# Last attention of a four-layer model: row maxima over pairs of banks, one exponential per bank, one output projection for two head groups

## The reference, cut to what matters

```
def _L3_xattn_ref(query, key, value, mask, Wq, bq, Wk, bk, Wv, bv, Wo, bo):
    Q = query @ Wq.T + bq; K = key @ Wk.T + bk; V = value @ Wv.T + bv
    ...
    scores = jnp.einsum('bhqd,bhkd->bhqk', Q, K) / jnp.sqrt(jnp.float32(DK))
    scores = jnp.where(mask == 0, -jnp.inf, scores)
    weights = jax.nn.softmax(scores, axis=-1)
    attn = jnp.einsum('bhqk,bhkd->bhqd', weights, V)
    return attn.transpose(0, 2, 1, 3).reshape(b, -1, D) @ Wo.T + bo
```

## Time and profile before

| | us |
|---|---|
| median of 3 runs (lowest, highest) | 2823.01 (2810.94, 2833.49) |
| the profiled execution | 2821.8 |
| its span, first to last instruction | 2820.0 |

### The profile page before, as it was taken

How to read it: one execution, slowest core, us unless ns; L and a number is a source line. 1 busy time by engine, 2 the same in 40 slices (tenths; PEclk the granted TensorE clock), 3 DMA queues, 4 the chain that set the end, 5 groups by cost and what they waited for, 6 DMA issues and landing times.

```text
span 2820.0 us, 32986 instructions
## 1 busy us (share of the span) xinstructions
PE 2473.9 (88%) x12476; PEld 1269.9 (45%) x12476; DVE 1821.0 (65%) x3631; ACT 1196.4 (42%) x1580; POOL 509.5 (18%) x281
## 2 busy tenths in 40 slices
PE   8999999998767884999897999885999999999878
PEld 3322222223322233778664677663444444443377
DVE  5676777887568766233453244483786888887386
ACT  2343433434345431122441223450365666666753
POOL 0333333333222226200002540000000000000011
PEclk8999999999869997999997999885697999999989
DMA  3000000000020004100102220003130202000042
GB/s 117 1 1 1 1 1 1 1 1 1 12 120 1 0 1 160 59 1 1 37 32 87 82 70 1 4 1 75 42 56 1 36 6 37 6 31 1 1 147 93
DMA packets 47866, 93.49 MB, mean 33 GB/s; under 512 B 7211, under 2 KB 32441, under 8 KB 46681
## 3 DMA queue, kind: packets, MB, share of 16 engines
q1 hardware_dynamic: 47078, 90.22, 10.4%
q10 hardware_dynamic: 628, 1.14, 0.2%
HBM read 79.48 MB, written 11.38 MB: 32 GB/s over the span
## 4 chain that ended last, share of the span: by engine, by line
PE 55%; DVE 13%; ACT 3%; issue 2%; DMA 2%; ACTq 0%; SPq 0%; POOL 0%; DVEq 0%; POOLq 0%
PE PS L2374 7%; PE PS L1297 6%; PE PS L2355 5%; DVE pm L2479 4%; PE PS L2317 4%; PE PS L914 4%; PE PS L1255 2%; PE PS L1278 2%; PE PS L1280 2%; PE PS L1279 2%; PE PS L896 1%; PE PS L2398 1%; PE PS L373 1%; DVE xg L324 1%; PE PS L1072 1%
## 5 line engine op out<-in xcount | busy, mean ns | idle before, releaser
L2479 DVE TENSOR_REDUCE pm<-PS 128x1 f32<-128x512 f32 x768 | 479.3, 684 | 100.5 <-PE PS L2317 100.4
L2445 ACT ACTIVATE P<-PS 128x1024 f32<-128x1024 f32 (+1 forms) x416 | 407.7, 1021 | 213.8 <-PE PS L2355 212.2
L2317 PE MATMUL PS<-Ks,Qs 49*128 49x512 f32 x768 | 314.8, 491 | 41.3 <-DMA Qs<-row 26.5
L682 ACT ACTIVATE P<-PS 128x1024 f32<-128x1024 f32 (+1 forms) x208 | 212.7, 1024 | 319.3 <-PE PS L597 296.5
L714 DVE TENSOR_REDUCE pm<-PS 128x1 f32<-128x400 f32 (+1 forms) x512 | 265.2, 563 | 74.6 <-PE PS L563 72.2
L2355 PE MATMUL PS<-Qs,Ks 51*128 51x512 f32 (+1 forms) x832 | 281.0, 451 | 8.6 <-ACT P L2445 8.6
L2374 PE MATMUL PS<-P,V 128*17 128x512 f32 (+1 forms) x1664 | 231.7, 630 | 0.3 <-ACT P L2445 0.3
L610 PE MATMUL PS<-P,V 128*64 128x512 f32 (+1 forms) x832 | 227.2, 625 | 4.9 <-ACT P L682 4.9
L2355 PEld LDWEIGHTS PS<-Qs,Ks 51*128 51x128 f32 (+1 forms) x832 | 140.5, 191 | 191.3 <-ACT P L2445 148.6
L520 POOL TENSOR_TENSOR odd<-odd,P 128x1024 f32<-128x1024 f32 x64 | 164.6, 2572 | 257.3 <-ACT P L682 257.3
L2317 PEld LDWEIGHTS PS<-Ks,Qs 49*128 49x128 f32 x768 | 136.3, 198 | 138.3 <-DVE pm L2479 91.1
(11 more groups left out here) (343 smaller groups left out, 4673.7 us busy)
## 6 DMA issues: line engine op xcount, KB each, us to landing
mi<-in_mask SPq DMA_DIRECT2D x32, 800.5 KB, 4.4
We<-in_L_ffn_w SPq DMA_DIRECT2D x16, 1024.0 KB, 7.1
Wg<-gate_rows SPq DMA_DIRECT2D x8, 1024.0 KB, 11.8
Qs<-q_parts SPq DMA_DIRECT2D x90, 64.0 KB, 2.4
Ks<-k_parts SPq DMA_DIRECT2D x24, 200.1 KB, 6.5
q_parts<-T SPq DMA_DIRECT2D x7, 512.0 KB, 2.8
k_parts<-Tk SPq DMA_DIRECT2D x6, 400.0 KB, 2.5
X<-in_x SPq DMA_DIRECT2D x4, 512.0 KB, 8.4
```

The source lines that it names most:

```text
L682: e.activation(self.P[0:r, n % 4, :, :], PS[0:r, b:b + 2, :], ACT.Exp, scale=0.125).then_inc(*k.ac_exp.up(("A", n)))
L2317: m = e.matmul(PS[:, b, :], self.Qs[rows, s, pr, q0:q0 + 128], self.Ks[rows, s, pr, cs], start=True, stop=not masked)
L2445: e.activation(self.P[0:r, n % 4, :, :], PS[0:r, b:b + 2, :], ACT.Exp, scale=0.25).then_inc(*k.ac_exp.up((3, n)))
L2479: e.tensor_reduce(self.pm[:, u % 2, i, c:c + 1], PS[:, ring.of(("max", key)), :], AX.X, ALU.max).then_inc(*k.dv_max.up((3, *key)))
```

## The change

- **Maxima over two banks.** The ring becomes `[4, 6]`: a step takes one of two pairs of banks (4 and 5, 6 and 7). Two maxima matmuls of the same `hh` fill a pair, and one VectorE reduction reads 1024 columns: key blocks 0 and 1 of one query block, or key block 2 of two query blocks; `"rest"` pairs likewise (528 columns). The matmuls stay the same in number; VectorE's reductions per unit go from 48 + 4 to 24 + 2. A small step takes a whole pair of banks too.
- **One exponential per bank.** Scores use banks 0, 1 and 2 by turns; each of the four scores of a round has its own exponential of 512 columns, and waits for the exponential three scores earlier. The attend sum moves to bank 3. The order of the scores in a round is now both of `hh = 0`, then both of `hh = 1`.
- **Attend in the middle.** Attend of a round moves from the end of the next round to its middle, between the scores of `hh = 0` and those of `hh = 1`.
- **Projection for two head groups.** The attend results of groups 0 and 1 (2 and 3) are stacked on partitions 0 to 63 and 64 to 127 of `On3`, and `"wo"` runs once for both with 128 rows: 32 steps instead of 64, none in the rounds of units 1 to 4 and 9 to 12. `"back"` uses ordinary float32 matmuls with the identity in place of transposes.
- The prologue ahead of the first round and the slots of the small steps are laid out in blocks of four maxima steps.

```diff
-        self.ring = k.ring([4, 5, 7])
+        self.ring = k.ring([4, 6])
...
+        tiles = [[(pr, qt, c) for c in range(2)] for pr in range(2) for qt in range(4)]
+        tiles += [[(pr, qt, 2) for qt in (q, q + 1)] for pr in range(2) for q in (0, 2)]
+        out = [(self, "max", (u, *x, hh)) for two in tiles for hh in (1, 0) for x in two]
+        return out + [(self, "rest", (u, pr, hh)) for hh in (1, 0) for pr in range(2)]
...
-        out = [(self, "wo", (u, qt)) for qt in range(4)]
+        out = [(self, "wo", (u, qt)) for qt in range(4)] if u // 4 % 2 else []
...
+            slots = spread(weave(*parts), 13)
             for kt in range(KT):
+                for hh in range(2):
+                    for pr in range(2):
+                        out.append((self, "score", (u, kt, pr, hh)))
+                        if done < len(maxima):
+                            out.append(maxima[done])
...
+                    if hh == 0 and before:
+                        out.append((self, "attend", before))
...
+            n = 4 * (13 * u + kt) + 2 * hh + pr
+            rows, ps = slice(64 * hh, 64 * hh + 51), PS[0:r, n % 3, :]
...
+            if n > 2:
+                at.wait_ge(k.ac_exp, (3, n - 3))
...
-            at.wait_ge(k.ac_exp, (3, 2 * n + 1))
+            at.wait_ge(k.ac_exp, (3, 4 * n + 3))
...
-                m = e.transpose(PS[0:64, b, qt * 128:(qt + 1) * 128], self.OT[:, u % 2, qt, :], k.identf[:])
+                m = e.matmul(PS[self.rows(u), b, qt * 128:(qt + 1) * 128], self.OT[:, u % 2, qt, :], k.identf[:],
+                             start=True, stop=True)
...
-            e.activation(self.P[0:r, n % 4, :, :], PS[0:r, b:b + 2, :], ACT.Exp, scale=0.25).then_inc(
-                *k.ac_exp.up((3, n)))
+            e.activation(self.P[0:r, (2 * (n // 4) + pr) % 4, hh, :], PS[0:r, n % 3, :], ACT.Exp,
+                         scale=0.25).then_inc(*k.ac_exp.up((3, n)))
...
+            ps = PS[:, b:b + 2, :] if c == 2 else PS[:, b:b + 2, :].rearrange("p b n -> p (b n)")
             at.wait_ge(k.pe_max, (3, *key))
+            e.tensor_reduce(out, ps, AX.X, ALU.max).then_inc(*k.dv_max.up((3, *key)))
+            ring.freed["max", first] = (k.dv_max, (3, *key))
```

More of the change, by code:

```diff
@@ L2152, in max_steps, with second @@
     def max_steps(self, u):
-        return [(self, "max", (u, pr, qt, c, hh)) for pr in range(2) for qt in range(4) for c in range(3)
-                for hh in (1, 0)] + [(self, "rest", (u, pr, hh)) for pr in range(2) for hh in (1, 0)]
+        tiles = [[(pr, qt, c) for c in range(2)] for pr in range(2) for qt in range(4)]
+        tiles += [[(pr, qt, 2) for qt in (q, q + 1)] for pr in range(2) for q in (0, 2)]
+        out = [(self, "max", (u, *x, hh)) for two in tiles for hh in (1, 0) for x in two]
+        return out + [(self, "rest", (u, pr, hh)) for hh in (1, 0) for pr in range(2)]
+    def second(self, key):
+        u, pr, qt, c, hh = key
+        return (c == 1 or c == 2 and qt % 2), (u, pr, qt if c < 2 else qt // 2 * 2, 0 if c < 2 else 2, hh)
     def rows_steps(self, u):
@@ L2160, in key_loads, with blocks @@
         return [(self, "key stack", (g, hh, blk)) for hh in range(2) for blk in range(3)]
+    def blocks(self, maxima, rest, rows):
+        blocks = [maxima[i:i + 4] for i in range(0, len(maxima), 4)]
+        others = spread(rest, 10) + [[]] * len(blocks)
+        out = []
+        for block, steps in zip(blocks, others):
+            out += (block if block[0] else rows) + steps
+        return out
     def query_loads(self, g, c):
@@ L2179, in order @@
         maxima = [s for u in range(16) for s in self.max_steps(u)]
-        out += weave((maxima[:52] + self.rows_steps(0) + maxima[52:52 + ahead], 0.0, 1.0), (rest, 0.0, 0.7))
+        out += self.blocks(maxima[:52] + [None] * 4 + maxima[52:52 + ahead], rest, self.rows_steps(0))
         done = 52 + ahead
@@ L2197, in order @@
                 parts.append((next_load, 0.1, 0.2))
-            slots = [[]] * 2 + spread(weave(*parts), 36) + [[]]
+            slots = spread(weave(*parts), 13)
             for kt in range(KT):
[L2200 to L2217, removed]
+                for hh in range(2):
[3 more added lines that the diff above has]
+                            out.append(maxima[done])
+                            if maxima[done][1] == "rest" and maxima[done][2][1:] == (1, 0):
+                                later = self.rows_steps(maxima[done][2][0])
+                            done += 1
+                    if hh == 0 and before:
+                        out.append((self, "attend", before))
+                        if before[1] == KT - 1:
+                            out.append((self, "take", before[:1]))
+                out += later[:2] + slots[kt]
+                later = later[2:]
                 before = (u, kt)
@@ L2220, in order, with rows @@
         return [s for s in out if s]
+    def rows(self, u):
+        return slice(64 * (u // 4 % 2), 64 * (u // 4 % 2) + 64)
     def stored(self, key):
@@ L2312, in tensor @@
             masked = step == "max masked"
-            b = ring.take(at, ("max", key))
+            last, first = self.second(key)
+            b = ring.of(("max", first)) + 1 if last else ring.take(at, ("max", key))
             at.wait_ge(self.ld_row, "all")
@@ L2326, in tensor @@
             masked = step == "rest masked"
-            b = ring.take(at, ("rest", key))
+            b = ring.of(("rest", (u, 0, hh))) + 1 if pr else ring.take(at, ("rest", key))
             for qt in range(4):
```

69 lines of the change are left out of this document (33 added, 36 removed).

## The result

| | before | changed |
|---|---|---|
| median, us | 2827.2 (20 runs, 2810.9 to 2839.8) | 2853.0 (20 runs, 2841.3 to 2874.8) |
| ratio | 1 | 1.010, 95% interval 1.0083 to 1.0118 |
| profiled execution: time, span, mean granted clock | 2821.8, 2820.0, 0.915 | 2844.5, 2842.6, 0.908 |

The change costs 1.0%, 28 us by the ratio and 26 by the medians. The forecast was 2824 us in a range of 2796 to 2856: the time lies in the range, 3 us under its upper end, and the sum of +1 us is short by nearly all of it.

A forecast was written before the change was run, and what follows sets the result against it. It took a TensorE-VectorE loop of 2.70 us a round as the bound. Units without projections -18, units with them +10, last 16 rounds +7, prologue +1, end +1: +1 on 2823.0 gives 2824 us, range 2796 to 2856.

The forecast's parts named there:

- Plain rounds: Rounds without small steps in the last attention: 2.65 us each against 2.70, set by a loop between TensorE and ScalarE.
- The reduction: VectorE's maxima over 1024 columns: 1.22 us alone and 1.14 in a row, 2.3 a round.
- Rival D: A reduction over two banks costs more than two of today's; at 1.4 us each, +27 us: 2851; chance 0.04.
- Rival A: VectorE sets the pace of rounds, say 2.35 us each, 64 us less: about 2755 us; chance 0.08.
- Small steps: Rounds with a divide, back, turn or projection: 3.67 us, 1.0 more than plain; units of 37.5 or 41.5 us.
- rival C: Clock falls in units 1 to 4 go with their projections, giving back 13 and 6 us: 2805; chance 0.18.
- The last 16 rounds: Rounds without maxima at the end: held at 2.65 us by the new loop, +7 us.
- The recorded signs of being wrong: Plain rounds under 2.5 or over 2.8 us, or granted clock changing by over 0.05 in a 100 us stretch.
- Rival B: More waiting lowers TensorE's clock in units 5 to 8 and 13 to 15: +38 us, 2862; chance 0.13.
- Prologue and end: Prologue before the first round: +1 us, between -2 and +5; unit 15's steps amid the next network: +1, 0 to +2.
- within 1%: Whole kernel's time within about 28 us of no change: chance 0.73.
- dearer exponentials: By the skill's figures two exponentials take 1.13 us for 1.08, a round 2.70: some 5 us added to the sum.

## Why the prediction was right and wrong, step by step

**Plain rounds: right in size, one piece wrong.** Forecast 2.65 us, measured 2.65, and VectorE left the chain as foretold. But the forecast's loop had one score and two exponentials (0.49 + 1.08) between two attends. The real one has two scores and one exponential (0.44 + 0.61 + 0.04 + 0.49): attend waits for its place in TensorE's order behind a score, and this score for its bank. The two paths happen to be equally long at 2.4 GHz, so the number held. At 1.2 GHz they are not, and the bound by banks is what five banks remove and what moving attend doesn't.

**The reduction: right.** This is the row of its line in the changed kernel (durations least, median and most):

```profile
L2503 DVE TENSOR_REDUCE pm<-PS x384: 1211/1224/1229, 1945.6 to 2609.9; 128x1 f32<-128x1024 f32 x128, 128x2 f32<-128x1024 f32 x64
```

1.22 us as forecast, in a row 2.35 to 2.36 for two, so the second adds 1.13 to 1.14 (1.14 forecast). Rival D, two banks dearer than that, falls. Rival A falls too: VectorE doesn't set the pace of the plain rounds, it waits 0.30 us in a round of 2.65 (some 0.4 were forecast).

**Small steps: right without projections, too cheap with them.** Rounds with one take mostly 3.7 us (3.67 forecast); a unit without projections takes 38.1 (37.5). Units 5 to 8 take 42.6, 44.3, 45.2 and 41.3, mean 43.4 (41.5), where the kernel before has 39.6: 15 us more for the four, twice the 7 that 1.7 each gave. Rounds with a projection cost up to 5.4 us where the next transposes or loads meet them, which "1.0 more than a plain round" for all had left out. Units 13 and 14 took 50.8 and 51.9, but 47.7 and 43.2 before, so their difference of 12 us is far from the +3.4 that two units at 1.7 gave; the last three rounds of unit 14 are already of the last 16, with the low clock.

**Units 1 to 4: rival C came true in its time.** They took 40.1, 44.4, 52.0 and 40.7 us before, 177 in all, and 38.1 each after, 152.5. Of these 25 us the clock gave back 18 (177 less four units of 39.8), which C had priced at 19. In the new order the projections are what matters: undone, the clock went back to 0.82 and units 2 and 3 to over 51 us. They are not the only way, though. The old kernel with attend in the middle keeps all its projections and has 1.00 in that stretch, and with split exponentials the same four units took 171.6 instead of 177 (one profiled execution each). So C's mechanism is shown for the changed kernel, not for why the old one falls.

**The last 16 rounds: the step that failed.** The forecast was +7 us, measured +34 from the last maximum to the last attend. The step took the loop of 2.65 us and multiplied it, at 2.4 GHz. The loop part was about right (+10 in the kernel with unread matmuls); what was missing is that the clock, once fallen at the pause for the norm's table loads, stays down in these rounds, 24 us of the 34. The recorded signs of being wrong caught it: they name a granted clock that changes by over 0.05 in a stretch, and it went from 0.87 to 0.52 here and from 0.85 to 1.00 in units 1 to 4. Rival B had this mechanism (more waiting, lower clock) and put it in the units full of small steps. There the clock held, 0.99 from 2200 to 2555; it went in the last rounds, which have no maxima. The Trainium skill (TensorE: Matmul & The Clock Gate, A second HAM failure mode: psum-queue depth-cycling) says that frequent small idle times between groups of matmuls make the clock go up and down, which costs throughput. This case agrees in part: the two kernels with attend behind all scores and three banks do go up and down in this stretch (low for 44 and 14 us in one, 14, 20 and 14 in the other), but the changed kernel shows one fall that lasts 92 us.

**Prologue and end.** +1.3 us for +1. The end was +4.3 for +1: TensorE went into the next stage with its clock still down, until 2709, 15 us past the last attend.

**Sum.** Body -11 with what C gave, last rounds +34, ends +6, part not touched -6: +23 in the profiled pair, +26 between the medians. Without the stuck clock, which is 24 of it in the last rounds, the change comes to no difference, as the unread matmuls measured (0.9997). The forecast's chance of "within 1%" was for that, and the 1.0% measured is at its edge; C's gain and B's mechanism both came, and the second was the larger. That the time lies in the range at all is luck: without C's 18 us, which the sum did not hold, it would have been some 2871 (an estimate, 2853 + 18), outside. One small sum of the forecast is low, without weight: 0.05 us more a round for dearer exponentials, put at some 5 us, is 7 us over its own 132 rounds without small steps.

**What stays open.** Why the last rounds get the clock back in the old kernel with attend in the middle, after a wait of 0.69 us, and in the changed kernel don't, with 0.26 in each round. TensorE was busy for 5.31 of 6 us there, and for 74.50 of 80 here. Three banks don't explain it either: two kernels above get the clock back with three, and so does the one with 64 projections, whose attend stands in the middle as in the changed kernel (low for 55 us, then up):

```profile
2768.00:2777.00 9.00, 7.44 (x39) 2.28 (x38) 3.62 (x15) 7.77 (x13) 0.00 (x0) 1.00 0.00 0
```

That the low clock lasts was shown to be the cause of 24 us, and matmuls that nobody reads bring it back; by what rule it lasts was not shown. The reductions over two banks, with their ring of two pairs for three single banks, and the new form of `"back"` were never undone alone, so what they bring or cost by themselves is open too.

## What to carry to other kernels

Price the rounds in which an engine's side work has run out by themselves, and at both of TensorE's clock levels: a loop that waits a little in each round at 1.2 GHz may stay there for long. Look for a pause just ahead (here two table loads), and give the loop more banks as soon as they fall idle: in the last rounds five banks brought 20 us where moving attend had brought 5. Of a bundle of edits undo each alone: here the halved projections were worth 60 us in the new order, the split exponentials cost nothing in the old one, and the place of attend cost 27 us in the body, which the sum over all edits hid.

## What the runs showed of the hardware that was not expected

- TensorE stayed at its 1.2 GHz level for 92 us, in both profiled executions of the changed kernel, though it was busy for 74.50 of 80 us and waited only 0.26 us in a plain round of 4.04. In close variants with three banks such spells lasted 14 to 55 us.
- Some sixty matmuls whose results nobody reads made the kernel 1.0% faster: the last stretch went from 79.8 us to 55.8, its granted clock from 0.52 to 0.91.
- Exponentials of 512 columns follow each other every 0.48 to 0.49 us, one alone takes 0.60. The Trainium skill (ScalarE: Activation LUTs, What ACT_TABLE_LOAD costs) gives 186 ns and 0.833 ns an element with 93 ns of overlap for ACTIVATEs back to back. Worked out from these figures (an estimate), one alone takes 0.61 us, which agrees, one follows every 0.52, where the rows have 0.03 to 0.04 less, and four in a row take 2.17; the row of four above has 2.08.
- A reduction over two banks shows no penalty for crossing from one to the other: 1024 columns in 1.22 us, 1.05 ns for each column more than one of 512 has (0.684), the same as from 400 to 512 columns.
